# 128-wide attention: the queries' norm factor moved from four products per tile into the exponential's scale

## What is computed

```python
q = (draft_hidden @ Wq.T).reshape(bsz, draft_len, H, HD)
q = _rms_norm(q, q_norm_w).transpose(0, 2, 1, 3)
kv_in = jnp.concatenate([context_hidden, draft_hidden], axis=1)
k = (kv_in @ Wk.T).reshape(bsz, total_len, KVH, HD)
v = (kv_in @ Wv.T).reshape(bsz, total_len, KVH, HD).transpose(0, 2, 1, 3)
k = _rms_norm(k, k_norm_w).transpose(0, 2, 1, 3)
q = _rope(q, draft_position_ids)
k = _rope(k, full_position_ids)
scores = jnp.einsum('bhqd,bhkd->bhqk', q, k) * SCALE
probs = jax.nn.softmax(scores, axis=-1)
```

## Time and profile before

| what | value |
|---|---|
| median of 3 runs | 1111.87 us (1106.99 to 1112.99) |
| profiled execution, its own time | 1111.39 us |
| its span, first to last instruction | 1109.6 us |
| PE busy | 843.7 us (76%) |
| DVE busy | 708.0 us (64%) |
| ACT busy | 499.0 us (45%) |
| POOL busy | 399.7 us (36%) |
| `exps`, L798, 128 of them | 45.4 us, 378 ns each |

### The profile page before, as it was taken

The page is one execution under the profiler, slowest core; times in us unless marked ns, Lnnn a source line. Parts: engine busy times, 40 slices in busy tenths (PEclk is TensorE's granted clock), DMA queues, the critical chain, the costliest instruction groups (busy, mean ns, idle before and its releaser), DMA issues. The chain is left out here.

```text
span 1109.6 us, 17247 instructions
## 1 busy us (share of the span) xinstructions
PE 843.7 (76%) x5527; PEld 554.3 (50%) x5534; DVE 708.0 (64%) x1495; ACT 499.0 (45%) x1273; POOL 399.7 (36%) x364
## 2 busy tenths in 40 slices
PE   2995784333778616785788999888756999999997
PEld 2774662321666514563356666666633444444443
DVE  2772795655899823563788877787254556565654
ACT  0672441311555425662356555556343454444543
POOL 1110475375555457740544533343011222212120
PEclk9996896557999958996899999999867999999999
DMA  9900000222888612200000000000014444434341
GB/s 322 392 1 1 1 2 3 61 82 93 249 275 272 206 39 57 58 2 0 1 1 1 1 0 0 1 2 1 1 46 120 127 114 117 124 107 132 103 116 39
DMA packets 49347, 90.64 MB, mean 82 GB/s; under 512 B 7047, under 2 KB 30090, under 8 KB 48779
## 3 DMA queue, kind: packets, MB, share of 16 engines
q1 hardware_dynamic: 46218, 81.63, 23.6%
q0 software_dynamic: 3072, 8.30, 2.4%
HBM read 67.71 MB, written 22.29 MB: 81 GB/s over the span
## 5 line engine op out<-in xcount | busy, mean ns | idle before, releaser
L1199 POOL TENSOR_TENSOR m1ws<-m1raw,m1ws 128x768 f16<-128x768 f32 x33 | 55.0, 1668 | 218.9 <-ACT m1raw L1202 218.9
L733 POOL TENSOR_TENSOR xqr<-xqr,xt 128x512 f32<-128x512 f32 x48 | 61.2, 1275 | 140.1 <-DVE xt L1069 140.1
L1509 DVE TENSOR_TENSOR m1sg<-m1sg,m1Wb 128x512 f32<-128x512 f32 x66 | 61.1, 925 | 64.0 <-ACT m1sg L1427 53.2
L1469 PE MATMUL m1pg<-m1hs,m1ws 128*128 128x512 f16 x396 | 97.5, 383 | 3.9 <-PEq L58 3.9
L1480 PE MATMUL m1py<-m1ap,m1ws 128*128 128x512 f16 x396 | 96.3, 379 | 1.8 <-DVE m1ap L1521 1.8
L1469 PE MATMUL m1pu<-m1hs,m1ws 128*128 128x512 f16 x396 | 96.7, 380 | 0.0
L1431 ACT ACTIVATE m1ap<-m1ac 128x512 f16<-128x512 f32 x66 | 41.6, 630 | 115.9 <-DVE m1ac L1515 115.9
L1521 DVE TENSOR_TENSOR m1ap<-m1ac,m1ap 128x512 f16<-128x512 f32 x66 | 45.7, 692 | 45.9 <-ACT m1ap L1431 45.9
L1469 PEld LDWEIGHTS m1pg<-m1hs,m1ws 128*128 128x128 f16 x396 | 38.9, 98 | 51.4 <-issue 5.4
L1480 PEld LDWEIGHTS m1py<-m1ap,m1ws 128*128 128x128 f16 x396 | 38.5, 98 | 49.1 <-DVE m1ap L1521 2.8
L788 ACT ACTIVATE xsq<-xpr 128x512 f32<-128x512 f32 x48 | 28.8, 600 | 75.3 <-PE xpr L896 75.3
(11 more groups left out here) (318 smaller groups left out, 2093.5 us busy)
## 6 DMA issues: line engine op xcount, KB each, us to landing
m1Wb<-wt_dram SPq DMA_DIRECT2D x66, 256.0 KB, 3.9
m1raw<-in_m_w SPq DMA_DIRECT2D x33, 384.0 KB, 4.3
slots_in<-zeros SPq DMA_DIRECT2D x1, 8192.0 KB, 26.8
m0rg<-in_m_wgu SPq DMA_DIRECT2D x32, 256.0 KB, 3.8
m0xg<-slots_in SPq DMA_DIRECT2D x32, 256.0 KB, 3.7
slots_out<-m0yo SPq DMA_DIRECT2D x32, 256.0 KB, 2.9
m0rd<-in_m_wd SPq DMA_DIRECT2D x32, 128.0 KB, 3.2
xwo<-in_x_wo SPq DMA_DIRECT2D x1, 2048.0 KB, 17.5
```

The lines of the kernel that those rows point to most:

```text
L733: pool.tensor_tensor(blk, blk, t2[:, k % 2, :, :], ALU.add).then_inc(add_ok, 1)
L1199: pool.tensor_tensor(ws[:, u, 1, :], raw[:, u, :], ws[:, u, 0, :], ALU.subtract).then_inc(prep_ok, 1)
L1469: ins = pe.matmul(bank[:, :], part(ws, u, sw, c, which), hs[:, sh, c, CH * q:CH * q + CH], start=(k == 0), stop=(k == 5))
L1509: dve.tensor_tensor(sg[:, q, :], sg[:, q, :], Wb[:, u, CH * q:CH * q + CH], ALU.mult).then_inc(sw_ok, 1)
```

## The change

The four products `scale` 0 to 3 on the queries are left out: `xqr` is transposed as it is, and `turn_qk` 0 to 3 wait for the sum (`add_ok`) alone. The factor instead multiplies the scores inside the exponential, as its scale. The scores have (head pair, token) on the partitions while `xsr` has tokens on the partitions and heads in columns, so the factors must be rearranged: `turn_rq` does this with four matmuls of a 64-column piece of the identity with 8 columns of `xsr` each, into 16 columns of the bank that `turn_h` then also uses (`roots_of`), and `rq_out` copies them, times the softmax scale, to a new tile `xrq`. `maxes` multiplies the maxima by `-xrq` where it multiplied by a constant, and each exponential takes a column of `xrq` as its scale. Tile 0 has a turn of its own for it, so `FIRST_T` is 7, and the turn `T_H` now exists in the last `mixed` too.

```diff
+        rq = sb("xrq", [P, 2, XH])
...
-        FIRST_T, STEP_T = 6, 11
+        FIRST_T, STEP_T = 7, 11
...
+        def roots_of(bank):
+
+            return p_t[bank][:, DC, 0:XH]
...
+            def rq_out(j, u, bank, alone):
+
+                act.wait_ge(t_ok, j + 1)
+                ins = act.activation(rq[:, u, :], roots_of(bank), ACT.Copy, scale=XSCALE)
+                if alone:
+                    ins.then_inc(t_out, 1)
...
-                    ins = act.activation(E[:, c, :], p_s[k % 2][:, i, :], ACT.Exp, bias=nb[:, c:c + 1], scale=XSCALE,
+                    ins = act.activation(E[:, c, :], p_s[k % 2][:, i, :], ACT.Exp, bias=nb[:, c:c + 1], scale=rq[:, u, c:c + 1],
                                          accum_out=sm[:, c:c + 1])
...
+            def turn_rq(n, bank):
+
+                pe.wait_ge(sr_ok, n * 2 + 1)
+                for b in range(2):
+                    for par in range(2):
+                        ins = pe.matmul(roots_of(bank)[S * par:S * par + S, NP * b:NP * b + NP], ident[:, S * b:S * b + S],
+                                        sr[:, par:XH:2], start=True, stop=True)
+                return ins
...
-                pe.wait_ge(scaled, n * 6 + i + 1)
+                if i < 4:
+                    pe.wait_ge(add_ok, n * 6 + i + 1)
+                else:
+                    pe.wait_ge(scaled, n * 2 + i - 3)
                 pe.wait_ge(t_out, j - 1)
...
+                pe.wait_ge(t_out, base + T_H - 1)
+                ins = turn_rq(n1, bank(T_H))
                 if there(n + 2):
-                    pe.wait_ge(t_out, base + T_H - 1)
-                    turn_h(n + 2, u, base + T_H, bank(T_H))
+                    ins = turn_h(n + 2, u, base + T_H, bank(T_H))
+                ins.then_inc(t_ok, 1)
...
-                dve.wait_ge(sr_ok, n * 2 + i // 4 + 1)
+                dve.wait_ge(sr_ok, n * 2 + 2)
...
-                dve.tensor_scalar(nb[:, c], mx[:, c], -XSCALE, None, ALU.mult).then_inc(nb_ok, 1)
+                if type(n) is int and k == 0 and n in (0, NT - 1):
+                    dve.wait_ge(t_out, FIRST_T if n == 0 else (n - 1) * STEP_T + FIRST_T + T_H + 1)
+                dve.scalar_tensor_tensor(nb[:, c], mx[:, c], -1.0, rq[:, u, c], ALU.mult, ALU.mult).then_inc(nb_ok, 1)
```

More of the change, by code:

```diff
@@ L703, in attention128 @@
                  " scaled t_ok t_out s_ok max_ok nb_ok exp_ok rc_ok e_ok o_ok o_out proj_ok x_ok high_ok chigh_ok")
-        FIRST_T, STEP_T = 6, 11
+        FIRST_T, STEP_T = 7, 11
         T_K, T_P, T_Q, T_H = (0, 1), (2, 3, 4, 6), (5, 7, 8, 10), 9
         def turns(n, u):
[L712 to L719, removed]
+            return n * STEP_T + FIRST_T, lambda k: (u + k + 1) % 2
+        def roots_of(bank):
+            return p_t[bank][:, DC, 0:XH]
         block = m.stack.enter_context(nc.Block())
@@ L822, in early @@
                     qk_out(2 + i, i, i % 2)
+                rq_out(6, 0, 0, True)
             def mixed(n, u, n1, u1):
@@ L830, in mixed @@
                 square(n1, 2)
-                exps(n, 0)
+                exps(n, u, 0)
                 square(n1, 3)
-                exps(n, 1)
+                exps(n, u, 1)
                 square(n1, 4)
@@ L838, in mixed @@
                 o_copy(n, u, 0)
-                exps(n, 2)
+                exps(n, u, 2)
                 o_copy(n, u, 1)
                 square(n1, 6)
-                exps(n, 3)
+                exps(n, u, 3)
                 pt_copy(n, 2, base + T_P[2], bank(T_P[2]))
@@ L849, in mixed @@
                 qk_out(base + T_Q[2], 2, bank(T_Q[2]))
+                rq_out(base + T_H, u1, bank(T_H), not there(n + 2))
                 if there(n + 2):
@@ L852, in mixed @@
                 o_copy(n, u, 3)
-                if there(n + 2):
-                    act.wait_ge(t_out, base + T_H + 1)
-                qk_out(base + t_q(n, 3), 3, bank(t_q(n, 3)))
+                act.wait_ge(t_out, base + T_H + 1)
+                qk_out(base + T_Q[3], 3, bank(T_Q[3]))
             def late(n, u):
@@ L948, in early @@
             def early(n, u):
-                turn_h(0, 0, 0, 0)
+                turn_h(0, 0, 0, 0).then_inc(t_ok, 1)
                 pe.wait_ge(t_out, 1)
@@ L952, in early @@
                     if k == 2:
-                        turn_h(1, 1, 1, 1)
+                        turn_h(1, 1, 1, 1).then_inc(t_ok, 1)
                     if k == 4:
@@ L958, in early @@
                     turn_qk(0, i, 2 + i, i % 2)
+                pe.wait_ge(t_out, 5)
+                turn_rq(0, 0).then_inc(t_ok, 1)
             def mixed(n, u, n1, u1):
@@ L1083, in scale, with maxes @@
                 dve.tensor_tensor(blk, blk, bcast(sr[:, 4 * i:4 * i + 4], 2, XD), ALU.mult).then_inc(scaled, 1)
-            def maxes(n, k):
+            def maxes(n, u, k):
                 c = slice(4 * k, 4 * k + 4)
@@ L1118, in early @@
                 mean_square(0, 1)
-                for i in range(6):
+                for i in range(4, 6):
                     scale(0, i)
@@ L1124, in mixed @@
                 rope(n1, 1)
-                maxes(n, 0)
+                maxes(n, u, 0)
                 rope(n1, 2)
-                maxes(n, 1)
+                maxes(n, u, 1)
                 normalise(n, 0)
@@ L1136, in mixed @@
                     norm_a(n + 2, u)
-                maxes(n, 2)
-                scale(n1, 0)
-                maxes(n, 3)
+                maxes(n, u, 2)
+                maxes(n, u, 3)
                 normalise(n, 2)
@@ L1143, in mixed @@
                 normalise(n, 3)
-                scale(n1, 1)
                 if there(n + 2):
                     norm_b(n + 2, u)
-                for i in range(2, 6):
+                for i in range(4, 6):
                     scale(n1, i)
```

6 lines of the change are left out of this document (3 added, 3 removed).

## The result

| what | before | after |
|---|---|---|
| median of 20 runs each | 1110.4 us (1104.41 to 1115.21) | 1113.34 us (1108.91 to 1117.83) |
| profiled execution, its own time | 1111.39 us | 1111.72 us |
| its span | 1109.6 us | 1109.9 us |
| VectorE busy | 708.0 us | 692.4 us |
| ScalarE busy | 499.0 us | 511.0 us |

The ratio after to before is 1.0031, interval 1.0019 to 1.0044: 3.4 us slower, 2.1 to 4.9 (the medians lie 2.9 apart). That is within the half per cent of "no change", and the predicted 1113.0 is met. Four products a tile left VectorE, and the kernel became a little slower. What follows is about why, and about which terms of the sum were right.

The account below looks back on a forecast made before the run. Bound by a chain through TensorE, ScalarE and VectorE in attention128, 33.07 us a middle tile. Terms -2.2 + 1.9 + 0.5 + 1.4 = +1.6 us on the profiled 1111.39 gave 1113.0; range 1107.5 to 1117.5.

Parts of the forecast that it names:

- The column, +0.36 a tile: Exponential's scale read from a column: 0.09 us more each, four exps on the chain before `normalise(2)`, +0.36 us a tile.
- the second 0.36: Exps 3 in a middle tile: their own 0.36 us lengthening is covered, by 0.2 us, behind rope 5.
- The products, -0.12: Four query products removed from VectorE: of 2.7 us a tile some 0.12 lies on the chain, before `turn_qk(1)`.
- VectorE's 22 us: 32 fewer products of 0.68 us each: VectorE less busy by 22 us, with nothing to show for it.
- `rq_out`, +0.09: New 128x16 activation on ScalarE ahead of `h_out`: +0.09 us, on the chain.
- `turn_rq`, "just covered": Small matmuls ahead of `turn_h`: 0.28 us for eight rows; `turn_h`'s result there at 671.97, ScalarE free at 672.0.
- Rival 3: `turn_rq` doesn't overlap: 1.9 us instead of 0.28, +1.6 in each of seven tiles, 11 us, 1124; chance 0.07.
- The border: Border of a middle tile: +0.36 + 0.09 - 0.12, less 0.02 of rounding: +0.31 us, six times +1.9.
- The seventh tile: No `low`, but small matmuls and their copy on TensorE's path to the projection: +0.36 + 0.28 - 0.12, +0.5 us.
- the last: Last tile: `turn_probs(1)` waits for eight exps, +0.72; `turn_probs(3)` for eight more, of which 0.64 tell: +1.4 us.
- The start, -2.2: Tile 0: `turn_qk(4)` can start 2.8 us earlier, 1.6 if it meets TensorE's lower clock; middle taken, -2.2 us.
- The sum: Whole kernel: -2.2 + 1.9 + 0.5 + 1.4 = +1.6 us, added to the profiled execution's own time.

Follow-up runs that it names:

- the old order: Order of the kernels before and after: square 6 ahead of exps 3, rope 5 ahead of `normalise(3)`; before 1110.4 us, after 1113.34 us.
- a new one: Exps 3 before square 6, `normalise(3)` before rope 5, `low` ahead of the key products; on the kernel before 1104.01 us, on the changed kernel 1102.17 us.

## Why the prediction held, point by point

**The column, +0.36 a tile:** measured 0.37, twice. The bound above, from the copy with a scale column, was the right row. That the second 0.36 is covered behind rope 5 was right too: the gap before `turn_probs(3)` stayed at 1.60.

**The products, -0.12:** measured -0.16. The reason given fits the rows: without product 1 `turn_qk(1)` follows `turn_probs(3)` after 0.49 instead of 0.61, and itself takes 0.60 instead of 0.65. No run took product 1 away alone. The rest of the four products lay beside other work.

**VectorE's 22 us:** VectorE was busy for only 15.6 us less. Inside the stage it is 19.4 less: a product of 0.68 is followed by the next instruction after 0.61 (662.39 and 663.00 in the middle tile), and 32 times 0.61 is 19.5. Outside the stage, where the work is the same, VectorE was busy for 3.8 us more.

**`rq_out`, +0.09:** measured 0.08.

**`turn_rq`, "just covered":** this is the step that failed. The sum gave it 0.28 and a cover with 0.03 to spare; it put the end of `turn_h` off by 0.48 to 0.49, against a cover of 0.35 at most. Its eight rows took a little more (0.33 to 0.34), and two costs at its borders were left out: 0.09 of lead-in and 0.06 more in `turn_h`. A term that was taken as nothing was 0.16 a period. Rival 3, with the full 1.9, is far from this: the small matmuls do overlap.

**The border:** 0.37 + 0.08 + 0.16 - 0.16 = 0.45, measured 0.44 in the mean, predicted 0.31. The seventh tile +0.75 instead of +0.5, the last +1.57 instead of +1.4. TensorE's gaps before `turn_probs` 0 to 3 in the last tile, after; the earlier trace rows has two of them at 0.28 and 1.01:

```profile
782.56 0.66 PE L928 MATMUL xpt<-ident,xE 128*128 128x128 f32 x4 [2.93 <-DVE xE L1121]
784.32 1.11 PE L928 MATMUL xpt<-ident,xE 128*128 128x128 f32 x4 [1.10 <-DVE xE L1121]
...
793.10 0.66 PE L928 MATMUL xpt<-ident,xE 128*128 128x128 f32 x4 [1.79 <-DVE xE L1121]
795.13 0.66 PE L928 MATMUL xpt<-ident,xE 128*128 128x128 f32 x4 [1.37 <-DVE xE L1121]
```

**The start, -2.2:** it was more. TensorE's first turns of queries and its `turn_qk(4)` after, against the earlier trace rows (538.95 and 545.24 there), in a stage that began 1.23 us earlier:

```profile
534.28 1.04 PE L961 MATMUL xpt<-ident,xqr 128*128 128x128 f32 x8
...
537.04 0.40 PE L895 MATMUL xpt<-xsr,ident 128*64 128x8 f32 x8 [0.20 <-ACT xQT L763]
...
539.51 0.66 PE L961 MATMUL xpt<-ident,xqr 128*128 128x128 f32 x4 [0.51 <-DVE xqr L1105]
```

`turn_qk(4)` came 4.5 us earlier against the start of the stage, where 2 to 3 was said. The way to it has three parts, all counted from the start of the stage.

- From the keys' root, with which their products begin, to `turn_qk(4)`: 0.75 us in place of 3.12, so 2.4. This is the part that the prediction described. It put it at 2.8, since it let `turn_qk(4)` start at 542.45, 0.33 behind the root, while the product it waits for takes 0.68.
- From the end of rope 5 to that root: 3.1 us in place of 4.0. The prediction kept this at 3.9. GpSimd's `add` of rope 5 and the root behind it, in before and then in after:

```profile
538.30 1.72 POOL L733 TENSOR_TENSOR xqr<-xqr,xt 128x512 f32<-128x512 f32 x1 [1.67 <-DVE xt L1069]
539.98 2.10 POOL L738 TENSOR_TENSOR xsr<-xsv,neghalf 128x8 f32<-128x8 f32 x1
```

```profile
535.85 1.27 POOL L731 TENSOR_TENSOR xqr<-xqr,xt 128x512 f32<-128x512 f32 x1 [0.67 <-DVE xt L1091]
537.07 1.66 POOL L736 TENSOR_TENSOR xsr<-xsv,neghalf 128x8 f32<-128x8 f32 x1
```

The two took 1.72 and 2.10 us in all four kernels in which VectorE's products on tile 0 stand beside them, and 1.27 and 1.66 in the ten others. So 0.9 us of the gain is GpSimd's, freed by the products, and no term of the sum had it.

- Up to the end of rope 5: 24.6 us in place of 25.9. The work is the same; it took 24.6 in the three executions in which a stretch at half of TensorE's clock around 530 is missing, after's among them, and 25.7 to 26.5 in the ten others with the same order there.

Windows that begin 16 us into the stage, before and after, and for after one that begins 30 us in, to be held against the earlier trace rows (stretch, us, busy and rows, granted clock, DMA share, GB/s):

```profile
528.28:530.28 2.00, 1.78 (x5) 0.50 0.00 0
```

```profile
527.05:529.05 2.00, 1.49 (x7) 1.00 0.00 0
541.05:543.05 2.00, 1.26 (x9) 1.00 0.01 4
```

The stretch at half the clock around 543, which the prediction expected to meet `turn_qk(4)`, is there in all four kernels that have the products, and in none of the ten without them: with the waits for products the drop goes too. In three of these ten a stretch falls some 13 us later instead. That the earlier stretch, around 530, is missing in after is owed to no edit, since kernels with the same work up to there show it; what decides it is open. With the border of tile 0 taken out, the start is thus 2.5 to 3.2 us shorter in the four kernels of the old order that have no products and show the earlier stretch, and 4.4 in after's.

**The sum.** By the ratio the change costs 3.4 us, the sum said 1.6, the interval begins at 2.1. Of the difference six borders make 0.13 each, the seventh tile 0.25, the last 0.17: 1.2 us more; the start takes 0.3 to 2.2 us back. So the stage's own terms give 0.6 to 2.5, and some 1 to 3 us of the measured 3.4 are in no row that I read. With the earlier stretch of the clock, which 11 of the 14 executions have, the terms give 1.8 to 2.5, which reaches into the interval. The comparison of single profiles can't settle them: the stage began anywhere from 507.7 to 513.0 us in these kernels, whose work is the same until then. The forecast's number was closer than its terms, and that was luck. Two errors of size, `turn_rq` and the start, point in opposite directions, and the 1113.0 was built on before's profiled execution of 1111.39 us, 1.0 above the median of its 20 runs. So the time was met to 0.3 us, while the change was forecast at +1.6 and measured at +3.4.

## What to carry to other kernels

Taking work from an engine that isn't on the chain brought next to nothing here until the order was changed so that it was: the same four products were worth 0.16 us a tile in the old order and about 0.7 in a new one. That one took a move on ScalarE and two on VectorE together, and no run separates them. Look also at what the work slows on a neighbour: without the products on VectorE GpSimd's `add` and root in tile 0 were 0.9 us shorter. A per-partition column in place of a constant is paid by each activation, so put it where an instruction is long or few, not in sixteen short ones on the chain. When a step is to be covered, count the lead-in and the effect on its neighbours besides its own rows, above all where the cover is only a few hundredths.

## What was not expected of the hardware

- Eight rows of f32 matmuls of 128x64 weights and 8 columns cost 0.33 us until the next can follow, and 0.15 at their borders (0.09 ahead, 0.06 in the transposition behind).
- A VectorE instruction on 128x4 took 0.16 us with GpSimd idle and up to 0.78 to 0.80 beside GpSimd's `add` on 128x512; the `add` took 1.26 to 1.27 with little beside it and 1.72 to 2.05 beside a product, and VectorE's product on 128x512 took 0.69 alone and 1.70 beside the `add`.
- TensorE was granted half its clock around 31 us into the stage in the four kernels with products and in none of the ten without. A stretch around 17 us into it was missing in three executions of 14 without a difference in the work up to there.
